# A transformer layer's first feed-forward product from operands split in two rounded parts

## What is computed

```python
D, H, W, L, FF = 192, 12, 128, 2, 768
for l in range(L):
    a = _longformer_attn(x, att_mask, Wq[l], ..., W, G_IDX)   # band attention and one global token
    x = _ln(x + a, g1[l], beta1[l])
    h = relu(x @ W1[l].T + b1[l]) @ W2[l].T + b2[l]
    x = _ln(x + h, g2[l], beta2[l])
```

## Time and profile before

| | us |
|---|---|
| median of 3 runs | 925.27 |
| lowest and highest | 923.58, 925.45 |
| the profiled execution | 922.18 |
| its span in the trace | 920.4 |
| TensorE busy (share of the span) | 809.1 (88%) |
| mean granted TensorE clock | 0.95 of full speed |

### The profile page before, as it was taken

How to read it: one execution, slowest core, us unless ns; L and a number is a source line. 1 busy time by engine, 2 the same in 40 slices (tenths; PEclk the granted TensorE clock), 3 DMA queues, 4 the chain that set the end, 5 groups by cost and what they waited for, 6 DMA issues and landing times.

```text
span 920.4 us, 23724 instructions
## 1 busy us (share of the span) xinstructions
PE 809.1 (88%) x8467; PEld 621.0 (67%) x8467; DVE 602.1 (65%) x1897; ACT 565.5 (61%) x1558; POOL 592.1 (64%) x884
## 2 busy tenths in 40 slices
PE   4989998999999989999999899999998967886397
PEld 1767866666778676677786666777856646775396
DVE  3678855447988464569884643798845336898454
ACT  2768885347788842277888524778884213665164
POOL 3549986544499865365998644349986445668245
PEclk9899999999999979999999899999998995999599
DMA  2320000602000006030000060200000623001231
GB/s 65 100 52 3 4 17 7 196 1 82 2 4 4 19 27 196 5 101 17 3 4 17 7 196 0 81 2 4 4 2 2 196 74 133 1 11 44 87 102 33
DMA packets 38596, 43.85 MB, mean 48 GB/s; under 512 B 7162, under 2 KB 33881, under 8 KB 38345
## 3 DMA queue, kind: packets, MB, share of 16 engines
q1 hardware_dynamic: 18348, 19.40, 7.1%
q10 hardware_dynamic: 17860, 18.19, 6.6%
q0 software_dynamic: 2272, 4.74, 1.6%
HBM read 20.70 MB, written 21.59 MB: 46 GB/s over the span
## 4 chain that ended last, share of the span: by engine, by line
PE 53%; POOL 13%; DVE 10%; issue 9%; ACT 6%; SPq 4%; DMA 3%; ACTq 1%; POOLq 0%; DVEq 0%
PE bank L1353 7%; POOL p L568 7%; PE bank L1559 4%; PE bank L1490 4%; PE bank L1560 4%; PE bank L1514 3%; PE bank L1379 3%; PE bank L1441 3%; PE bank L1390 3%; PE bank L1660 2%; PE bank L1669 2%; PE bank L1493 2%; DVE p L1002 2%; SPq L453 2%; POOL p L575 2%
## 5 line engine op out<-in xcount | busy, mean ns | idle before, releaser
L568 POOL TENSOR_TENSOR p<-p 128x384 f16<-128x384 f32 (+1 forms) x320 | 282.1, 902 | 67.2 <-ACT p L739 64.6
L737 ACT ACTIVATE p<-bank 128x384 f32<-128x384 f32 (+1 forms) x384 | 171.1, 452 | 56.8 <-PE bank L1493 41.4
L994 DVE TENSOR_REDUCE nmx<-bank 128x1 f32<-128x384 f32 (+1 forms) x384 | 192.5, 512 | 18.3 <-PE bank L1444 15.3
L1490 PE MATMUL bank<-stack 103*128 103x128 bf16 x1056 | 144.7, 221 | 2.8 <-DMA stack<-mtr 2.2
L739 ACT ACTIVATE p<-bank 128x384 f16<-128x384 f32 (+1 forms) x320 | 144.1, 450 | 0.0
L1493 PE MATMUL bank<-bandb,idb 128*128 128x128 bf16 x672 | 135.1, 221 | 0.0
L1514 PE MATMUL bank<-vst,p 128*128 128x49 bf16 x2112 | 116.5, 185 | 12.9 <-DVE p L1002 10.9
L1441 PE MATMUL bank<-stack 100*128 100x384 bf16 (+1 forms) x384 | 120.5, 314 | 4.7 <-DVE nmx L994 2.1
L1514 PEld LDWEIGHTS bank<-vst,p 128*128 128x128 f16 x2112 | 90.7, 97 | 27.8 <-DVE p L1002 16.4
L1490 PEld LDWEIGHTS bank<-stack 103*128 103x128 bf16 x1056 | 88.0, 98 | 27.3 <-issue 15.4
L540 POOL TENSOR_TENSOR rstd<-ve,colc 128x1 f32<-128x1 f32 x64 | 35.2, 550 | 107.6 <-DVE ve L916 107.6
(11 more groups left out here) (253 smaller groups left out, 1832.2 us busy)
## 6 DMA issues: line engine op xcount, KB each, us to landing
xs<-zrow ACTq DMA_DIRECT2D x8, 2193.0 KB, 12.4
xt<-xs SPq DMA_DIRECT2D x23, 129.0 KB, 2.1
w2s<-in_w SPq DMA_DIRECT2D x4, 576.0 KB
mwbs<-in_mwb SPq DMA_DIRECT2D x1, 2064.0 KB, 9.3
mw2s<-in_mw SPq DMA_DIRECT2D x1, 2048.0 KB, 13.6
lnrow<-in_lnr SPq DMA_DIRECT2D x4, 480.0 KB
stack<-mtr SPq DMA_DIRECT2D x96, 3.0 KB
w1b<-in_w SPq DMA_DIRECT2D x4, 291.0 KB
```

Of the source, the lines that this page charges most:

```text
L568: nc.gpsimd.tensor_tensor(p2[:, u % RING, 0:w], p32[:, u % RING, 0:w], p1[:, u % RING, 0:w], ALU.subtract).then_inc(p2_pool, 1)
L737: ins = nc.scalar.activation(p32[:, s % RING, 0:w], ps[2 + s % 3][:, 0:w], ACT.Exp)
L994: nc.vector.tensor_reduce(nmx[:, vn % 3, h:h + 1], nat_bank(v)[:, 0:w], AX.X, ALU.max, negate=True).then_inc(max_done, 1)
L1490: ins = mm(ps[2 + s % 3][:, blk(i)], stack[0:K_ALL, H + h, blk(m)], stack[0:K_ALL, h, blk(n)], start=True, stop=m == n)
```

## The change

The first feed-forward product is taken from operands that are split: a part rounded to the type float32r and the rest, also float32r. Of the four partial products three are computed, for both row groups, so that six products of 512 columns stand for two. The smaller operand parts are made so:

- ScalarE writes, in `tr` 0 to 3, the rounded part `xha`, `xhb` beside `xa`, `xb` (four instructions of 128 columns in place of two). For the second half of the tokens it makes them in the step `split` 4 with two copies of 512 columns, behind h_mm of tile 5.
- VectorE makes the rests `xla`, `xlb` by subtraction, in new steps of the list: `split` 0 to 3 (two subtractions of 128 columns each) and `split` 4 (two of 512). TensorE's `hid` waits for these (`x_split`) in place of `ln_out`.
- GpSimd rounds and subtracts the weights, in two parts, in the projection stage: w1's first 96 rows at j = 3 (copy) and j = 4 (subtraction), the other 97 at j = 6 (copy) and j = 7 (subtraction). Each is 768 columns wide and stands at the end of its j, ahead of the early steps.
- SyncE brings the raw weights into the tail of `hid`: the first part ahead of `load_rest`, the second behind it, behind the constants in round 0, and behind a wait for GpSimd's first subtraction. GpSimd waits for the landing of the second part at j = 6.
- In the list, tr4 and tr5 move ahead of hid0, and hid0 to hid5 stand together.
- The clearing transfers are issued at step `y` 9, behind ScalarE's copies of `split` 4.

```diff
-                                 (w1a[:, :], a[0:DLO, :]), (w1b[0:DHI + 1, :], a[DLO:D + 1, :]),
...
+            def load_w1(l, k):
+                w = w1[bass.ds(l, 1), :, :].rearrange("o k n -> (o k) n")
+                half = w[DLO:D + 1, :] if k else w[0:DLO, :]
+                sp.dma_start(w1raw[0:half.shape[0], :], half).then_inc(w1_in, 16)
...
+                    load_w1(l, 0)
                     load_rest(l)
                     if rnd == 0:
                         for dst, src in consts:
                             sp.dma_start(dst, src).then_inc(const_in, 16)
+                    sp.wait_ge(w1_split, at(w1_split, 1))
+                    load_w1(l, 1)
...
+                        if j == 3:
+                            pool.wait_ge(w1_in, at(w1_in, 16))
+                            ch.link(nc.gpsimd.tensor_copy(w1ha[:, :], w1raw[0:DLO, :]))
+                        if j == 4:
+                            nc.gpsimd.tensor_tensor(w1la[:, :], w1raw[0:DLO, :], w1ha[:, :].bitcast(F32),
+                                                    ALU.subtract).then_inc(w1_split, 1)
+                        if j == NB - 2:
+                            pool.wait_ge(w1_in, at(w1_in, 32))
+                            ch.link(nc.gpsimd.tensor_copy(w1hb[0:DHI + 1, :], w1raw[0:DHI + 1, :]))
+                        if j == NB - 1:
+                            nc.gpsimd.tensor_tensor(w1lb[0:DHI + 1, :], w1raw[0:DHI + 1, :], w1hb[0:DHI + 1, :].bitcast(F32),
+                                                    ALU.subtract).then_inc(w1_split, 1)
...
+                            if i < BPC:
+                                full = (xha[:, blk(n)], *full[0]), (xhb[0:DHI, blk(n)], *full[1])
...
+                        if kind == "split" and i == BPC:
+
+                            act.wait_ge(h_mm, at(h_mm, FF // P))
+                            act.wait_ge(ln_out, at(ln_out, NB))
+                            nc.scalar.activation(xha[:, :], xa[:, CH:T], ACT.Copy)
+                            nc.scalar.activation(xhb[0:DHI, :], xb[0:DHI, CH:T], ACT.Copy).then_inc(x_high, 1)
+                        if kind == "y" and i == NB + 1:
...
+                                act.dma_start(xs[e * REGION:(e + 1) * REGION, :].rearrange("(r p) w -> p r w", p=P),
...
-                            if i == 2:
...
+                        nc.vector.tensor_tensor(xla[:, here], xa[:, there], xha[:, here].bitcast(F32), ALU.subtract)
+                        nc.vector.tensor_tensor(xlb[:, here], xb[0:DHI, there], xhb[0:DHI, here].bitcast(F32),
+                                                ALU.subtract).then_inc(x_split, 1)
...
-                            pe.wait_ge(ln_out, at(ln_out, (c + 1) * BPC))
+                            pe.wait_ge(x_split, at(x_split, BPC + c))
...
-                            mm(ps[6 + i % 2][:, :], w1a[:, m * P:(m + 1) * P], xa[:, cs], start=True, stop=False)
-                            mm(ps[6 + i % 2][:, :], w1b[0:DHI + 1, m * P:(m + 1) * P], xb[0:DHI + 1, cs], start=False,
-                               stop=True).then_inc(h_mm, 1)
+                            mm(h, w1ha[:, ms], xha[:, :], start=True, stop=False)
+                            mm(h, w1ha[:, ms], xla[:, :], start=False, stop=False)
+                            mm(h, w1la[:, ms], xha[:, :], start=False, stop=False)
+                            mm(h, w1hb[0:DHI + 1, ms], xhb[0:DHI + 1, :], start=False, stop=False)
+                            mm(h, w1hb[0:DHI, ms], xlb[:, :], start=False, stop=False)
+                            mm(h, w1lb[0:DHI + 1, ms], xhb[0:DHI + 1, :], start=False, stop=True).then_inc(h_mm, 1)
...
+            seq.append(("split", i))
...
-    seq.append(("tr", 3))
+    seq += [("tr", 3), ("split", 3)]
     y(7)
-    seq.append(("z", 7))
-    seq += [("hid", m) for m in range(3)] + [("tr", 4), ("tr", 5)] + [("hid", m) for m in range(3, 6)]
+    seq += [("z", 7), ("tr", 4), ("tr", 5)]
+    seq += [("hid", m) for m in range(6)]
     seq += [("tr", 6), ("tr", 7)]
-    seq += [("y", 8), ("y", 9), ("z", 8), ("y", 10), ("z", 9), ("y", 11), ("z", 10), ("z", 11)]
+    seq += [("y", 8), ("split", BPC), ("y", 9), ("z", 8), ("y", 10), ("z", 9), ("y", 11), ("z", 10), ("z", 11)]
```

More of the change, by code:

```diff
@@ L11 @@
 F32 = mybir.dt.float32
+F32R = mybir.dt.float32r
 BF16 = mybir.dt.bfloat16
@@ L199, in program @@
             hid = lsb("hid", [P, FF // P, CH], F32)
+            xha = lsb("xha", [DLO, CH], F32R)
+            xla = lsb("xla", [DLO, CH], F32R)
+            xhb = lsb("xhb", [P, CH], F32R)
+            xlb = lsb("xlb", [DHI, CH], F32R)
+            w1ha = lsb("w1ha", [DLO, FF], F32R)
+            w1la = lsb("w1la", [DLO, FF], F32R)
+            w1hb = lsb("w1hb", [P, FF], F32R)
+            w1lb = lsb("w1lb", [P, FF], F32R)
         h0 = sb("h0", [P, NN, DM], F32)
@@ L329, in program @@
         ln_out = sem("ln_out")
+        x_high = sem("x_high")
+        x_split = sem("x_split")
+        w1_in = sem("w1_in")
+        w1_split = sem("w1_split")
         h_mm = sem("h_mm")
@@ L371, in program @@
                  wq_ready)),
-            (2, (f_exp,)),
+            (2, (f_exp, w1_split)),
+            (32, (w1_in,)),
+            (BPC + 1, (x_split,)),
+            (1, (x_high,)),
             (NB, (qk_mm, v_mm, qk_hi, qk_rest, qk_mid, qk_lo, qk_again, v_hi, v_rest, v_mid, v_lo, sg_mm, mt_mm, m_hi, m_rest,
@@ L685, in _, with norm_out @@
             act.drain().then_inc(setup, 1)
-            def norm_out(j, k, dst, gb):
+            def norm_out(j, halves, gb):
                 act.wait_ge(z_mm, at(z_mm, j + 1))
                 bank = ps[4 + j % 2]
-                for i, (d, (g, o)) in enumerate(zip(dst, gb)):
-                    ins = nc.scalar.activation(d, bank[0:d.shape[0], i * P:(i + 1) * P], ACT.Identity, bias=o, scale=g)
+                for i, (dst, (g, o)) in enumerate(zip(halves, gb)):
+                    for d in dst:
+                        ins = nc.scalar.activation(d, bank[0:d.shape[0], i * P:(i + 1) * P], ACT.Identity, bias=o, scale=g)
                 ins.then_inc(ln_out, 1)
@@ L789, in _ @@
                             k, n = i // NB, block_of(i)
-                            norm_out(i, k, (xa[:, blk(n)], xb[0:DHI, blk(n)]),
-                                     ((lna[:, 2 * k:2 * k + 1], lna[:, 2 * k + 1:2 * k + 2]),
-                                      (lnb[0:DHI, 2 * k:2 * k + 1], lnb[0:DHI, 2 * k + 1:2 * k + 2])))
+                            full = (xa[:, blk(n)],), (xb[0:DHI, blk(n)],)
+                            if i < BPC:
+                                full = (xha[:, blk(n)], *full[0]), (xhb[0:DHI, blk(n)], *full[1])
+                            norm_out(i, full, ((lna[:, 2 * k:2 * k + 1], lna[:, 2 * k + 1:2 * k + 2]),
+                                               (lnb[0:DHI, 2 * k:2 * k + 1], lnb[0:DHI, 2 * k + 1:2 * k + 2])))
+                        if kind == "split" and i == BPC:
[4 more added lines that the diff above has]
+                        if kind == "y" and i == NB + 1:
+                            per = E // (B * L)
+                            act.wait_ge(late_ready, 1)
+                            for e in range(rnd * per, (rnd + 1) * per):
+                                act.dma_start(xs[e * REGION:(e + 1) * REGION, :].rearrange("(r p) w -> p r w", p=P),
+                                              zrow[:, :].unsqueeze(1).to_broadcast([P, REGION // P, RW])).then_inc(zeroed, 16)
                         if kind == "hid":
@@ L1059, in _, with split @@
                     dve.wait_ge(gathered, 16 * NB * (b + 1))
+                    def split(i):
+                        if i < BPC:
+                            n = block_of(i)
+                            dve.wait_ge(ln_out, at(ln_out, i + 1))
+                            here, there = blk(n), blk(n)
+                        else:
+                            dve.wait_ge(x_high, at(x_high, 1))
+                            here, there = slice(0, CH), slice(CH, T)
+                        nc.vector.tensor_tensor(xla[:, here], xa[:, there], xha[:, here].bitcast(F32), ALU.subtract)
+                        nc.vector.tensor_tensor(xlb[:, here], xb[0:DHI, there], xhb[0:DHI, here].bitcast(F32),
+                                                ALU.subtract).then_inc(x_split, 1)
                     for kind, i in seq_c(rnd):
+                        if kind == "split":
+                            split(i)
                         if kind == "hid" and i == 0 and rnd + 1 < B * L:
```

16 lines of the change are left out of this document (9 added, 7 removed).

## The result

| | median of the runs, us | lowest to highest | profiled execution, us (span) | mean granted clock |
|---|---|---|---|---|
| before | 924.42 (4 runs beside the changed kernel) | 922.07 to 925.45 | 922.18 (920.4) | 0.950 |
| changed | 948.96 (4 runs) | 945.87 to 949.72 | 949.34 (947.6) | 0.924 |

The ratio is 1.0264, with a 95% interval from 1.0243 to 1.0286: 24.5 us slower. I had said 929.2 us, in a range of 920.5 to 938.5. The sign was right; the time lies 10 us above the upper end of the range.

What follows compares the result with a forecast made beforehand. TensorE was taken to bound the feed-forward, VectorE's statistics to pace just before hid0. Terms -4.4 (feed-forward), +7.5 (round 0) and +0.8 (rounds 1 to 3) gave +3.9: 926.1 us profiled, 929.2 median, range 920.5 to 938.5.

Steps and rivals of the forecast that it cites:

- Rounds 1 to 3: W1's second part arrives in time; small delays of GpSimd's gather and L1465: 0.8 us lost for all three (0 to 2).
- about nothing: Later rounds' projection stage: GpSimd's last subtraction delays `egh` to 240.4, ended by 240.65, where L1465 stood at 240.91.
- Round 0: GpSimd waits for W1's second part behind the constants, making TensorE late: 7.5 us lost (5.5 to 9.5).
- the second rival: Round 0: SyncE gets through the constants sooner without w1b ahead, so GpSimd's wait doesn't reach TensorE: 921.7 us; chance 0.06.
- the clock: Granted clock falls at TensorE's gap ahead of hid0: 1.8 us lost a round (0 to 3.4); 0.4 more at the start.
- The product: Feed-forward tiles: six one-pass products of 512 columns, 0.215 us each, replace two f32 products of 0.86 us.
- The third rival: Feed-forward: float32r isn't one-pass and runs at 0.43 us a product: +41, about 975 us; chance 0.05.
- The second half: hid6 to hid11: splits and clearing transfers covered by y8 to y11; 2.6 us gained a round.
- The first half: hid0 to hid5: split not covered, hid0 4.2 us later; 0.3 gained less 1.8 for the clock, 1.5 lost a round.
- The sum: Whole kernel: -4.4 + 7.5 + 0.8 = +3.9 us on the profiled execution, so 926.1; median 929.2.
- The feed-forward: Both halves of the feed-forward together: 1.1 us gained a round, 4.4 in all.
- the four rivals: Clock costs nothing, 0.20; start's wait misses TensorE, 0.06; float32r not one-pass, 0.05; dear clock and splits, 940 us, 0.12.

Runs made afterwards that it cites:

- the cured kernel before: Kernel before, with its load of w1b issued as 96 rows and 1 row: 918.85 us, ratio 0.9959.
- The orders above: Three feed-forward work orders on the changed kernel with all 97-row loads cut into 96 and 1: 913.54, 912.91 and 901.71 us.
- the order with one split: Changed kernel, all 97-row loads cut, four products first, VectorE's eight 128-column subtractions made two of 512 behind y 7: 912.91 us.
- the hole filled: The order with one split, with split ahead of y 7 and first four products between transposes: 901.71 us; with GpSimd's late use of W1's second part also, 897.55.

## Why the prediction failed

**Rounds 1 to 3: the step that failed.** "The second part goes out some 9 us before j = 6 needs it" was about right (7.0 us in round 1: issued at 234.25, GpSimd ready at 241.3), and "about nothing" did not follow. I had priced the landing at 3.0 us from the earlier trace rows, whose transfers have 128 rows, and took kilobytes for what decides. It landed 14 us after its issue, and the wait was 7.0 to 7.7 us in each of the three rounds: +20.3 for +0.8. Cutting the load at row 96 took it away. The trace of before held the price in a row I didn't use: `wqb`, 97 rows and 218.2 KB by the trace's count (in which this load has 291.0), 12.97 us on the chain of waits, with the later rounds' load of it at 25 GB/s. Had I looked for the nearest row by shape and not by size, the bound would have been 12.97 x 291.0 / 218.2 = 17.3 us: some 8 us of wait in each of these three rounds, 25 in all, so that an upper end below 929.2 + 25 = 954 had no ground.

**Round 0: +7.5 predicted, +7.4 measured, by errors that cancel.** I had the issue at 57.2 and the landing 3.0 us later: 60.2. It was issued at 43.96, 13 us earlier, took five times as long, and GpSimd resumed at 58.63, 1.6 us before my time. The earlier issue is the second rival's mechanism, which I gave 0.06: SyncE's two long issues behind w1b were caused by it (the run of the cured kernel before shows this) and went with it. GpSimd's steps hold: cast, repeats, gather, subtraction and `egh` took 5.6 us for 5.4, and the transpose behind `egh` stood at 64.33, for 65.7 in my sum. The last step does not: from this transpose to the first attention step I took 2.9 us, as in the kernel before at full clock, and it took 4.5 (68.79 for 68.6). TensorE had been idle since about 55, and the granted clock was 0.50 from about 56 to about 70, so these products ran at half speed. I had let the clock fall only behind the wait, and taken 0.4 us for it.

```profile
63.97 0.22 POOL L582 TENSOR_TENSOR egh<-eg,egh 128x12 f16<-128x12 f32 x1
...
64.33 0.27 PE L1522 MATMUL bank<-idh,egh 128*24 128x128 f16 x1 [1.58 <-POOL egh L582]
...
68.79 0.37 PE L1547 MATMUL bank<-stack 103*128 103x128 bf16 x2
```

The stretches with TensorE alone:

```profile
56.00:58.00 2.00, 0.00 (x0) 0.52 0.08 28
58.00:60.00 2.00, 0.00 (x0) 0.50 0.00 0
...
68.00:69.00 1.00, 1.00 (x19) 0.50 0.00 0
```

A total that comes out right is no proof of its terms.

**The product.** 0.216 us was taken; 0.234 apart is what the rows show at full clock (180.31 and 180.55), so a tile costs 1.40 us for 1.30. With 12 tiles a round this is 1.2 us a round, some 5 in all. The third rival, 0.43 a product at full clock, is out.

**The second half.** The splits, the copies and the clearing transfers are covered by y8 to y11, as said. From y8 to the last relu it is 16.9 us for 18.8 in round 0: 1.9 gained for 2.6 predicted, and the difference is the product's.

**The first half.** Relative to y0, hid0 starts 4.2 us later (12.6 for 8.4): as predicted. The subtractions took 0.28 us, once in eight 0.34, and in every round the same two of eight 0.67, each beside GpSimd's update of the residual; others beside GpSimd's work took 0.28. The spread that I read in the earlier trace rows mixed two widths: at 384 columns alone it is 0.55 to 1.26 us, with GpSimd's subtraction beside both. From hid0 to y8 11.9 us were needed where I had 8.7 and 1.8 for the clock. Of the 1.4 us more, 0.6 is the product; the rest is the clock, at 0.50 until about 179, for over 5 us of tiles. At 0.43 a product for 0.234 this is some 2.5 us for the 1.8 taken. The orders above show this price from the other side.

**The sum.** The feed-forward: +2.2 for -4.4, 6.6 us off. In round 0 it is +1.0 for -1.1: 1.2 of these 2.1 us are the product's, 0.7 the clock's, 0.2 stay unassigned; the other rounds came out at -0.4, +0.9 and +0.7, and I did not take them apart. Rounds 1 to 3: 19.5 us off. Round 0: nothing. The other two stretches gave 2.7 us back, which I don't explain. That makes the 23.2 us by which the profiled execution (949.34 for 926.1) was missed. The median was missed by less, 19.8, for a reason that is no merit: I had added 3.1 us for the way from the profiled execution to the median, and the changed kernel's profiled execution lies 0.4 above its median. None of the four rivals held the mechanism that decided; the range left out that a landing can be five times the one taken.

## What to carry to other kernels

Price a transfer by the nearest row of the same row count, not of the same kilobytes: 97 rows took 14 us where 96 and 1 took under 4 (waits of 7 to 8 us gone), and a busy share that stays near 1/16 at some 25 GB/s is the mark of it in a trace, in the kernel before already. Before a wait is added on an engine, ask what stands behind it in that engine's queue, and whether the use can be put where the engine is idle: this alone gave back 25 us, with the transfer as slow as it was. And where TensorE falls idle ahead of a dense stretch, fill the hole from the list of work before making anything shorter: the order alone moved this kernel by 11 us.

## What the runs showed of the hardware

- A transfer's rate goes by its row count. 97 and 89 rows ran at some 25 GB/s (a DMA share of 0.06 to 0.07), 94 at 40 to 55 (0.11 to 0.14), and 96 moved at up to 258 GB/s (0.77, over half a microsecond).
- A transfer on one engine holds up the issues of the large transfers behind it on the same queue: 5.77 and 6.71 us behind 97 rows, 0.40 and 1.06 behind 96 and 1.
- Six products of float32r, 512 columns, are 0.234 us apart at the high clock (2.4 GHz) and 0.43 apart at the low one (1.2 GHz).
- In the order with one split, round 0, TensorE idled for 1.6 us from 156 to 158, and from about 159 on the granted clock was at 1.2 GHz for some 10 us, though TensorE was busy without a gap in nearly all of them. With the hole filled it stayed at 2.4 GHz in all eight rounds seen; with the hole it stayed there in one of eight.
- VectorE's subtractions of 128 columns with both operands in SBUF took 0.28 us, and 0.67 in the same two of eight places in each round.
